# One head transfer for two: W's first piece and PT's first four chunks loaded jointly, with eight warm-up matmuls

## The reference

```python
y = einsum('bti,oi->bto', x, W) + b                  # 2048 -> 2048
y = y + 2.0 * einsum('btr,bro->bto', einsum('bti,bir->btr', x, loraA[slot]), loraB[slot])
logits = einsum('bsd,ed->bse', y, route_w)           # 8 experts
h = einsum('bsd,erd->bser', y, A)                    # rank 16 for each expert
wh = onehot(argmax(logits)) * max(logits) * h
out = x + einsum('bser,eor->bso', wh, Bw)
```

## Time and profile before

| | before |
|---|---|
| median of 3 runs | 289.58 us (289.46 to 289.77) |
| profiled execution | 289.77 us |
| its span, first to last instruction | 288.0 us |
| TensorE matmul busy | 282.7 us, 98% |
| VectorE, ScalarE busy | 202.4 us, 112.6 us |
| mean granted TensorE clock | 0.996 |
| moved by DMA | 88.52 MB, mean 307 GB/s |

### The profile page before, as it was taken

One profiled execution on the slowest core, in us unless ns is written; L12 is line 12 of the kernel. 1 busy time (PEld: TensorE's weight loads), 2 busy tenths in 40 slices (PEclk: granted clock), 3 DMA queues, 4 the chain that ended last, 5 costly groups with the idle time before them and its releaser, 6 DMA issues.

```text
span 288.0 us, 4401 instructions
## 1 busy us (share of the span) xinstructions
PE 282.7 (98%) x1700; PEld 226.2 (79%) x1700; DVE 202.4 (70%) x234; ACT 112.6 (39%) x166; POOL 12.5 (4%) x44
## 2 busy tenths in 40 slices
PE   8999999999999999999999999999999999999994
PEld 5999999996766885888588758857885888588993
DVE  0061200077698998799789969896998798699974
ACT  0001300196877532744373355427432642443300
POOL 6300030000000000000000000000000000000000
PEclk9999999999999999999999999999999999999998
DMA  7999999999980247759958993999499769536668
GB/s 250 406 408 395 402 416 411 373 415 424 418 373 6 93 200 272 312 178 404 386 203 296 409 364 137 380 366 381 140 378 391 263 220 420 238 127 256 272 236 277
DMA packets 19591, 88.52 MB, mean 307 GB/s; under 512 B 2410, under 2 KB 5106, under 8 KB 11762
## 3 DMA queue, kind: packets, MB, share of 16 engines
q1 hardware_dynamic: 16128, 84.87, 75.7%
q10 hardware_dynamic: 3442, 3.37, 3.5%
HBM read 54.60 MB, written 33.55 MB: 306 GB/s over the span
## 4 chain that ended last, share of the span: by engine, by line
PE 98%; DVE 0%; DVEq 0%; issue 0%
PE bank_out L661 16%; PE bank_h L738 11%; PE bank_h L739 10%; PE bank_h L740 10%; PE bank_out L699 10%; PE bank_out L701 10%; PE bank_out L700 10%; PE bank_e L723 10%; PE bank_h L668 1%; PE bank_r L661 1%; PE bank_h L661 1%; PE bank_e L661 1%; PE bank_l L675 1%; PE bank_l L661 1%; PE bank_l L749 1%; PE bank_r L758 1%
## 5 line engine op out<-in xcount | busy, mean ns | idle before, releaser
L405 ACT ACTIVATE x_hi<-x_ring 128x1024 fp32r<-128x1024 f32 (+1 forms) x72 | 69.0, 965 | 66.7 <-PE bank_h L740 65.9
L507 DVE TENSOR_TENSOR x_lo<-x_ring,x_hi 128x1024 fp32r<-128x1024 f32 (+1 forms) x72 | 78.9, 1102 | 11.9 <-ACT x_hi L405 10.1
L598 DVE TENSOR_TENSOR x_ring<-bank_out,x_ring 128x1024 f32<-128x1024 f32 (+1 forms) x71 | 78.4, 1106 | 1.7 <-PE bank_out L701 1.2
L738 PE MATMUL bank_h<-x_hi,m_hi 128*128 128x512 f32 (+1 forms) x144 | 54.1, 376 | 0.0
L739 PE MATMUL bank_h<-x_lo,m_hi 128*128 128x512 f32 (+1 forms) x144 | 53.3, 370 | 0.0
L740 PE MATMUL bank_h<-x_hi,m_lo 128*128 128x512 f32 (+1 forms) x144 | 53.2, 369 | 0.0
L699 PE MATMUL bank_out<-wh_hi,bw_hi 128*128 128x512 f32 (+1 forms) x143 | 53.1, 371 | 0.0
L701 PE MATMUL bank_out<-wh_hi,bw_lo 128*128 128x512 f32 (+1 forms) x143 | 53.0, 371 | 0.0
L700 PE MATMUL bank_out<-wh_lo,bw_hi 128*128 128x512 f32 (+1 forms) x143 | 53.0, 371 | 0.0
L661 PE MATMUL bank_out<-pt,w_ring 128*128 128x136 f32 x384 | 46.0, 281 | 0.0
L661 PEld LDWEIGHTS bank_out<-pt,w_ring 128*128 128x128 f32 x384 | 45.4, 192 | 0.7 <-DMA w_ring<-W 0.7
(11 more groups left out here) (79 smaller groups left out, 162.3 us busy)
## 6 DMA issues: line engine op xcount, KB each, us to landing
x_ring<-xT SPq DMA_DIRECT2D x32, 1024.0 KB, 7.6
outT<-x_ring SPq DMA_DIRECT2D x28, 1024.0 KB, 4.8
w_ring<-W SPq DMA_DIRECT2D x30, 512.0 KB, 10.3
outT<-x_ring SPq DMA_DIRECT2D x12, 256.0 KB, 2.9
w_ring<-W SPq DMA_DIRECT2D x4, 256.0 KB, 4.5
x_ring<-loraB ACTq DMA_DIRECT2D x8, 128.0 KB, 10.3
la<-loraA ACTq DMA_DIRECT2D x8, 128.0 KB, 13.1
x_ring<-BwT SPq DMA_DIRECT2D x1, 1024.0 KB, 11.1
```

Of the source, the lines that this page charges most:

```text
L405: act.activation(out, in_, ACT.Copy).then_inc(done, 1)
L507: dve.tensor_tensor(out, a, b, ALU.subtract).then_inc(done, 1)
L598: dve.tensor_tensor(x, out_banks(u, j), x, ALU.add).then_inc(v_out, 1)
L738: mm(h, m_hi[:, c, :], hi, start=(c == 0), stop=False)
```

## The change

The host lays out a new input, `head`, of shape (2, 128, 784): for each half of W's piece 0, 512 floats of W (two chunks of 256 columns) followed by 272 floats of PT (two chunks of 136). SP loads it as two transfers of 392 KB into one tile, `head_sb`, each with a semaphore of its own (`d_head`). ACT issues no part of PT any more. PT's other twelve chunks come in the three parts as before. Only piece 1 is still loaded in halves. The matmuls of piece 0, the matmuls with loraB and the bias sums find their operands through `w_chunk` and `pt_chunk`. Slot 0 of the ring is empty until piece 8, which no longer waits for piece 0's matmuls. `bp` and `ones` get bytes of their own, outside the shared area. There are eight warm-ups instead of nine.

```diff
+    NHEAD = head.shape[0]
+    HO = WO // NHEAD
+    HEAD_W = HO * WI
-    PT_PARTS = [(0, 2), (2, 4), (4, 8), (8, 12), (12, 16)]
+    PT_PARTS = [(4, 8), (8, 12), (12, 16)]
-    HALVED = 2
-    PT_AFTER = {3: 2, 6: 3, 9: 4}
+    PT_AFTER = {3: 0, 6: 1, 9: 2}
...
-        pt = sb("pt", [P, C, PN], F32, phase1)
+        pt = sb("pt", [P, C - WO, PN], F32, phase1)
+        head_sb = sb("head_sb", [P, NHEAD, HEAD_W + HO * PN], F32, phase1)
-        bp = sb("bp", [P, XN], F32, phase1)
-        ones = sb("ones", [P, P], F32, phase1)
...
+        bp = sb("bp", [P, XN])
+        ones = sb("ones", [P, P])
...
+        def pt_chunk(c):
+
+            if c >= WO:
+                return pt[:, c - WO, :]
+            at = HEAD_W + c % HO * PN
+            return head_sb[:, c // HO, at:at + PN]
+
+        def w_chunk(n, o, i):
+
+            if n > 0:
+                return w_ring[:, n % WRING, o, i * P:(i + 1) * P]
+            at = o % HO * WI + i * P
+            return head_sb[:, o // HO, at:at + P]
+
+        def loads_in_slot(n):
+
+            return n // WRING + (1 if n % WRING else 0)
...
-        WARM_UP = 9
+        WARM_UP = 8
...
-                if n >= WRING:
+                if n > WRING:
                     sp.wait_ge(t_w, n - WRING + 1)
                 blk, part = ORDER[n]
-                if n < HALVED:
-                    sp.dma_start(w_ring[:, n, 0:WO // 2, :], W[blk, part, :, 0:WO // 2, :]).then_inc(d_w_first[n], 16)
+                if n == 0:
+                    for h in range(NHEAD):
+                        sp.dma_start(head_sb[:, h, :], head[h]).then_inc(d_head[h], 16)
+                elif n == 1:
+                    sp.dma_start(w_ring[:, n, 0:WO // 2, :], W[blk, part, :, 0:WO // 2, :]).then_inc(d_w_half, 16)
...
-            for k in range(2):
-                c0, c1 = PT_PARTS[k]
-                act.dma_start(pt[:, c0:c1, :], PT[:, c0:c1, :]).then_inc(d_pt[k], 16)
             act.dma_start(slots[:, :], slot_of).then_inc(d_slots, 16)
...
+                cuts = {0: range(0, WO + 1, HO), 1: (0, WO // 2, WO)}.get(n, (0, WO))
+                for o0, o1 in zip(cuts, cuts[1:]):
+                    if n == 0:
+                        pe.wait_ge(d_head[o0 // HO], 16)
+                    elif o1 < WO:
+                        pe.wait_ge(d_w_half, 16)
                     else:
-                        pe.wait_ge(d_w_first[n], 16)
+                        pe.wait_ge(d_w[n % WRING], 16 * loads_in_slot(n))
...
+                            last = mm(bank, w_chunk(n, o, i), pt_chunk(k), start=(k == 0), stop=(k == C - 1))
```

More of the change, by code:

```diff
@@ L44, with adaln_ffn @@
 NGROUPS = P // GROUP
-def adaln_ffn(nc, xT, slot_of, W, PT, bias, loraA, loraB, BwT, outT):
+def adaln_ffn(nc, xT, slot_of, head, W, PT, bias, loraA, loraB, BwT, outT):
     NPIECES, _, PIECE = xT.shape
@@ L124, in adaln_ffn @@
         wh = sb("wh", [P, T])
-        assert C * PN + NB * XN + 2 * XN + 2 * E + P + P // 2 <= 9 * T, "the second lot covers the first"
+        assert C * PN + HO * NHEAD * WI + NB * XN + XN + 2 * E + P // 2 <= 9 * T, "the second lot covers the first"
+        bp = sb("bp", [P, XN])
+        ones = sb("ones", [P, P])
         pb_sum = [sb(f"pb_sum{i}", [P, PN]) for i in range(2)]
@@ L167, in adaln_ffn @@
         d_pt = [sem(f"d_pt{i}") for i in range(NPT)]
-        d_w_first = [sem(f"d_w_first{n}") for n in range(HALVED)]
+        d_head = [sem(f"d_head{h}") for h in range(NHEAD)]
+        d_w_half = sem("d_w_half")
         d_w = [sem(f"d_w{i}") for i in range(WRING)]
@@ L318, in _ @@
                     c0, c1 = PT_PARTS[k]
-                    sp.dma_start(pt[:, c0:c1, :], PT[:, c0:c1, :]).then_inc(d_pt[k], 16)
+                    sp.dma_start(pt[:, c0 - WO:c1 - WO, :], PT[:, c0:c1, :]).then_inc(d_pt[k], 16)
                 if n == 7:
@@ L528, in _ @@
             for c in range(C):
+                if c < WO and c % HO == 0:
+                    dve.wait_ge(d_head[c // HO], 16)
                 for k in range(NPT):
@@ L532, in _ @@
                 if c == 0:
-                    dve.tensor_scalar(pb_sum[0][:, :], pt[:, 0, :], bias_sb[:, 0:1], None, ALU.mult).then_inc(v_pb, 1)
+                    dve.tensor_scalar(pb_sum[0][:, :], pt_chunk(0), bias_sb[:, 0:1], None, ALU.mult).then_inc(v_pb, 1)
                 else:
                     dve.wait_ge(v_pb, c)
-                    dve.scalar_tensor_tensor(out=pb_sum[c % 2][:, :], in0=pt[:, c, :], scalar=bias_sb[:, c:c + 1],
+                    dve.scalar_tensor_tensor(out=pb_sum[c % 2][:, :], in0=pt_chunk(c), scalar=bias_sb[:, c:c + 1],
                                              in1=pb_sum[(c - 1) % 2][:, :], op0=ALU.mult, op1=ALU.add).then_inc(v_pb, 1)
@@ L660, in w_piece @@
                                     pe.wait_ge(d_pt[p], 16)
-                            last = mm(bank, w_ring[:, n % WRING, o, i * P:(i + 1) * P],
-                                      pt[:, k, :], start=(k == 0), stop=(k == C - 1))
+                            last = mm(bank, w_chunk(n, o, i), pt_chunk(k), start=(k == 0), stop=(k == C - 1))
                 last.then_inc(t_w, 1)
@@ L674, in _ @@
             for c in range(C):
-                last = mm(bank_l[:, 0:PN], lb_cols[:, c, :, :].rearrange("p b r -> p (b r)"), pt[:, c, :],
+                last = mm(bank_l[:, 0:PN], lb_cols[:, c, :, :].rearrange("p b r -> p (b r)"), pt_chunk(c),
                           start=(c == 0), stop=(c == C - 1))
@@ L793 @@
     rows = np.where(turned[:, 0] == 1, turned[:, 2] + turned[:, 1] + 1, turned[:, 2]) % e * r + half // e * turned[:, 0] + turned[:, 1]
+    weights = W.reshape(dout // (wo * P), wo, P, din // wblock, wblock).transpose(3, 0, 2, 1, 4)
+    factors = np.concatenate([route_w, A.reshape(e * r, dout)[rows]]).reshape(e * r + e, dout // P, P).transpose(2, 1, 0)
+    head = np.concatenate([
+        a.reshape(P, 2, -1).transpose(1, 0, 2) for a in (weights[0, 0], factors[:, :wo])], axis=2)
     arrays = {
@@ L797 @@
         "slot_of": slot_of.reshape(1, nb),
-        "W": W.reshape(dout // (wo * P), wo, P, din // wblock, wblock).transpose(3, 0, 2, 1, 4),
-        "PT": np.concatenate([route_w, A.reshape(e * r, dout)[rows]]).reshape(e * r + e, dout // P, P).transpose(2, 1, 0),
+        "head": head,
+        "W": weights,
+        "PT": factors,
         "bias": bias.reshape(dout // P, P).T,
```

## The result

The changed kernel takes 287.14 us (median of 6, 286.74 to 287.52) against 289.58: 0.9915 of the time before, 95% interval 0.9902 to 0.9927. I forecast 289.49 within 289.04 to 289.92. That is a gain of 2.44 us where I expected 0.09, and it is faster where I gave "same" 0.77.

The account below looks back on a forecast made before the run. The prediction took TensorE, busy 98% of the span, to bound the kernel. A start 0.18 us earlier, worth half, gave -0.09 us and all else nothing: 289.49 us from 289.58, range 289.04 to 289.92.

Parts of the forecast that it names:

- The tiles that moved out of the shared area cost space only: On bp and ones getting bytes of their own: no effect on time.
- my rivals: At the start: joint transfer no quicker (0.22), clock later (0.08), clock sooner (0.10), full clock in timed runs (0.10).
- What bounds the kernel: Whole span: TensorE, busy 98%, hardly held up after its first real matmul, so changes at the start arrive undiminished.
- The joint transfer: First load of W and PT: lands at 4.45, so TensorE streams from 4.75, 0.18 us sooner.
- My floor: Earliest landing of the first joint transfer: 4.54 less 0.37 us for PT's 136 KB, 4.17.
- The second joint transfer: Second half of piece 0, needed at 6.07: in time with 0.4 us cover; at worst +0.34 us.
- what lies behind: Loads after the joint transfers: piece 2 and all later ones keep their time, none waited for.
- the halving by the clock: Before the clock rise at about 5.78, time gained is worth half: 0.18 us sooner counts as -0.09 us.
- the sign of a wrong prediction: In the profile after: the clock rise moving by more than a microsecond either way.
- My fourth rival: Timed runs have full clock when real work starts, so nothing is halved: 289.04 to 289.40, chance 0.10.
- The later rise, at 9.54: Rival at the start: longer idle gap delays the clock rise by 3.76 us, +1.88 us, 291.4, chance 0.08.
- Room, not gain: Eight warm-ups end at 4.39 instead of 4.81, but data hold the first real matmul until 4.75.

Follow-up runs that it names:

- layout_only: Kernel before with only bp and ones moved out of the shared area, tiles behind 1088 bytes later: 287.37 us, ratio 0.9929.
- after_shift_2048: Changed kernel with 960 spare bytes per partition behind ones, tiles behind 2048 bytes later than in the kernel before: 289.63 us, ratio 1.0007.
- after_pad_64: Changed kernel with 64 spare bytes behind ones, tiles behind 1152 bytes later than in the kernel before: 286.11 us, ratio 0.9883.
- before_pad_128_again: Repeat of the kernel before with 128 spare bytes ahead of pb_sum, shifting the tiles behind the shared area: 286.26 us, ratio 0.9890.

## Why the prediction was wrong

**The step that failed** is the sentence "The tiles that moved out of the shared area cost space only", with the claim ahead of it that another tile for the first four chunks changes neither shape nor count. Shape and count are as I said. But 1088 bytes of shift changed the distance between the weights and the streamed tiles, and TensorE's pace in the streaming phase depends on it: 1.74 us over six batches, 2.5 from batch 0's block to the end. layout_only has this without anything else, after_shift_2048 has everything else without this. It was not among my rivals: all four lay at the start.

**What bounds the kernel** was right, and it is why the miss is large: with TensorE packed to the end, 3 ns on each of some hundred matmuls a batch arrive undiminished.

**The joint transfer** was mis-sized in a direction that I had excluded. I took a landing of 3.7 us after issue and a floor of 3.43 (4.17 less 0.74); it was 2.8 to 3.1. My floor subtracted from W's half only the time of PT's bytes beside it, and left in the packets of the second pair of transfers that ran between; that this is the reason was not tested. I then gave the Trainium skill's fixed part plus bytes (DMA: Bandwidth & Descriptors, the two cost components) as a rule against the change, at 0.32 us more than the traced half piece. Its own figure for 392 KB, an estimate of 2.0 + 0.92 = 2.9 us, agrees with the traces (2.8 to 3.1) when the transfer is the first of SP's queue and ACT sends only the slot list, although the page gives that fit for transfers that GpSimd issues. It did not describe the two queues of before: by it 256 KB take an estimated 2.6 us, and the traces have 3.2 to 3.9. That interleaving is the cause of the late PT pair was only argued; no run separated it.

**The second joint transfer and "what lies behind"** failed in the profile after. I had everything behind keep its time without a wait; there are now waits of 0.17 and 0.32 us on pieces 1 and 2. Piece 1's halves land 4.2 and 4.9 us after issue, the first of them sooner than the 4.7 of before, but TensorE comes for them sooner still. So the gain at the start is capped by the stream of W. The joint transfers end in no measurable gain (after_shift_2048 at 1.0007, and the 0.15 us between after_pad_64 and before_pad_128_again). My -0.09 us for this part thus agrees with the runs by luck: I had the halving by the clock where the wait for W was.

**The clock.** The halving is real where the clock is low at the start, as in the profile before. It is not a fixed 4.79 us after the first warm-up: in the profile after it came near 3.65 us with the same warm-ups up to there. That is 2.1 us from 5.78, more than the microsecond that I had named as the sign of a wrong prediction, though it is not what made the number wrong. My fourth rival (full clock at the start of real work) is what that profile shows. The later rise, at 9.54, is in no profile: worked out from the spacing, the rise lies between 3.7 and 5.5 us in the five with joint transfers and between 3.9 and 6.3 in the fourteen without. Within that it moves between executions by more than the change could move it.

**Where the first matmul starts.** I read 4.93 for the kernel before from the weight loads. The trace records the first real matmul at 4.80, as the ninth warm-up ends, and the second at 5.15, 0.35 later instead of 0.23. The idle 0.12 us is the same, but by these starts it lies behind the first matmul.

**Eight warm-ups.** "Room, not gain" holds for the kernel before: 0.9993. In the changed kernel's profile it was the other way round, with data at 3.74 and the warm-ups through at 4.02, so the ninth would have cost there; that cost then went into the wait for W, and with nine the loss is below what the runs can tell.

## What to carry to other kernels

If a change moves any tile, check the addresses behind it before pricing it: here a spare tile of 128 bytes is worth 3.3 to 3.6 us of 289.6, more than anything that was changed at the start. When a phase that the diff does not touch changes its pace, compare the same count of instructions over the same stretch in both traces, and undo the layout alone first. A transfer that lands sooner helps only as far as the next pieces of the same stream do.

## What the runs showed of the hardware

The pace of full-length fp32r matmuls, with TensorE never idle and at the upper clock, depends on where the weights lie relative to the tiles that are streamed: six batches take 157.72 us with a shift of 128 bytes, 159.04 with 64, 160.74 with 0 or 2048, 161.29 with 32, and 160.74 again when all tiles move together. Where only x meets the folded matrix, moving either against the other has the whole effect (15.64 us to 15.50 with 64 bytes, to 15.42 with 128). The Trainium skill (TensorE: Matmul & The Clock Gate, Step-by-step: what each phase is for) says that the weights of the next matmul are read through a port of their own, so that loading them takes no bandwidth from the running one; if nothing at all were shared, moving the weights alone could not change the pace, and it does. What stays open: the rule behind 0, 32, 64, 96, 128, 192; why the parts (the folded matrix, the bw tiles, x_hi and x_lo together) do not add up to the whole where both kinds of matmuls alternate; and whether DVE's and ACT's accesses beside the matmuls take part, which no run tried.

The step of TensorE's clock from its lower to its upper level came near 3.65 us in one profile and at 5.78 in another with the same warm-ups up to there, about 1 us of run time by the halving (an estimate).
